# The last feed-forward of a GNN block: two tiles weighed inside the first part's loop, the first turning ahead of the last first product, and no filling products

## The reference

```python
input_acts = _gelu(jnp.einsum('bsd,nd->bsn', x, input_patterns))         # 256 of 256 kept
process_acts = _gelu(jnp.einsum('bsn,pn->bsp', input_repr, process_input_weights))
top_p_acts, top_p_idx = jax.lax.top_k(process_acts, K_PROCESS)           # 128 of 1024
sel_values = process_values[top_p_idx]
p_weights = jax.nn.softmax(top_p_acts, axis=-1)
agg_value = jnp.einsum('bsk,bskd->bsd', p_weights, sel_values)
output_acts = _gelu(jnp.einsum('bsd,od->bso', agg_value, output_input_weights))
out = jnp.einsum('bsk,bskm->bsm', top_o_acts, sel_patterns)              # 256 of 256 kept
```

## Time and profile before

| what | value |
|---|---|
| median of 3 runs | 1284.91 us (1284.19 to 1285.83) |
| the profiled execution's own time | 1289.82 us |
| its span (first to last instruction) | 1288.1 us |
| TensorE busy | 1219.5 us, 95% |
| VectorE busy | 547.9 us, 43% |
| ScalarE busy | 452.7 us, 35% |
| GpSimd busy | 227.7 us, 18% |
| the last feed-forward's first product | at 1162.14 us of the span |
| the last output product | at 1280.97 us of the span |

### The profile page before, as it was taken

The page is one execution under the profiler, slowest core; times in us unless marked ns, Lnnn a source line. Parts: engine busy times, 40 slices in busy tenths (PEclk is TensorE's granted clock), DMA queues, the critical chain, the costliest instruction groups (busy, mean ns, idle before and its releaser), DMA issues. The chain is left out here.

```text
span 1288.1 us, 19378 instructions
## 1 busy us (share of the span) xinstructions
PE 1219.5 (95%) x6528; PEld 814.0 (63%) x6529; DVE 547.9 (43%) x1535; ACT 452.7 (35%) x965; POOL 227.7 (18%) x227
## 2 busy tenths in 40 slices
PE   4999899999999899999999999999989999989898
PEld 2555476468448555478877887786555587564465
DVE  8999743433443344110000000001296345675784
ACT  6878533233223310011111111111123343338873
POOL 1000070030000008311111111111273000025540
PEclk9999899999999989999999999999998999999899
DMA  9300000000003300671165312564562010100011
GB/s 221 91 1 1 1 2 1 0 2 2 0 6 126 130 2 1 203 273 42 44 245 182 115 44 70 216 236 148 167 186 98 1 35 1 74 0 1 1 31 52
DMA packets 42978, 98.25 MB, mean 76 GB/s; under 512 B 4142, under 2 KB 6632, under 8 KB 41874
## 3 DMA queue, kind: packets, MB, share of 16 engines
q1 hardware_dynamic: 28642, 68.70, 16.0%
q0 software_dynamic: 6144, 16.45, 4.6%
q10 hardware_dynamic: 8112, 12.08, 2.6%
HBM read 81.02 MB, written 16.17 MB: 75 GB/s over the span
## 5 line engine op out<-in xcount | busy, mean ns | idle before, releaser
L498 PEld LDWEIGHTS psum<-sb_blk,sb_w_reg 128*128 128x128 f32 x1792 | 204.0, 192 | 12.8 <-issue 12.8
L498 PE MATMUL psum<-sb_blk,sb_w_reg 128*128 128x128 f32 x1792 | 205.2, 275 | 1.7 <-issue 1.7
L2145 PE MATMUL psum<-sb_z_reg_r,sb_hT_conv_r 125*125 125x512 f32 x385 | 156.9, 408 | 0.4 <-DVE sb_z_last L1262 0.4
L1434 DVE TENSOR_TENSOR sb_blk<-sb_blk,psum 128x256 f32<-128x256 f32 x56 | 23.6, 421 | 277.0 <-ACT sb_blk L955 277.0
L2145 PE MATMUL psum<-sb_htok_r,sb_hT_conv_r 125*125 125x512 f32 x285 | 112.9, 396 | 0.0
L498 PE MATMUL psum<-sb_hT_conv,sb_w_reg 128*128 128x416 f32 (+3 forms) x336 | 103.6, 465 | 0.8 <-ACT sb_hT_conv L532 0.8
L2235 PE MATMUL psum<-sb_w_reg,sb_blk 128*128 128x512 f32 x224 | 100.8, 592 | 0.0
L498 PEld LDWEIGHTS psum<-sb_hT_conv,sb_w_reg 128*128 128x128 f32 x336 | 63.8, 193 | 35.9 <-issue 33.0
L2145 PEld LDWEIGHTS psum<-sb_z_reg_r,sb_hT_conv_r 125*125 125x125 f32 x385 | 72.0, 187 | 18.0 <-issue 0.7
L2067 PE MATMUL psum<-sb_w_reg,sb_hT_conv 128*125 128x512 f32 x160 | 83.1, 613 | 0.0
L955 ACT ACTIVATE sb_blk<-psum 128x256 f32<-128x256 f32 x56 | 21.5, 384 | 162.9 <-PE psum L498 160.1
(11 more groups left out here) (452 smaller groups left out, 2002.3 us busy)
## 6 DMA issues: line engine op xcount, KB each, us to landing
sb_hT_conv<-w_expert SPq DMA_DIRECT2D x7, 2048.0 KB, 9.8
sb_w_reg<-w_expert SPq DMA_DIRECT2D x6, 2048.0 KB, 18.1
sb_hT_conv<-w_expert SPq DMA_DIRECT2D x7, 1024.0 KB, 12.4
slot_outs<-sb_blk ACTq DMA_DIRECT2D x28, 256.0 KB
sb_w_reg<-w_expert SPq DMA_DIRECT2D x6, 1024.0 KB, 19.9
sb_w_reg<-w_gnn SPq DMA_DIRECT2D x1, 4096.0 KB
sb_w_reg<-w_qkv SPq DMA_DIRECT2D x1, 3072.0 KB, 21.5
slot_outs<-sb_blk ACTq DMA_DIRECT2D x1, 2560.0 KB, 13.1
```

The source lines that it names most:

```text
L498: ins = e.matmul(out, l, r, start=(n == 0), stop=(n == len(pairs) - 1))
L1434: e.tensor_tensor(hidT[:, 2 * h:2 * h + 2, :].rearrange("p k n -> p (k n)"), silg[:, h, :], psum[:, 1 + h, HF:2 * HF], ALU.mult).then_inc( ...
L2145: ins = e.matmul(psum[0:TP, b, :], counts_at(l, 2 * i + n // NT)[:, s % HALF_T, :], z[s], start=(n == 0), stop=(n == len(pairs) - 1))
```

## The change

FIRST_PRODUCTS = 8. TensorE forms the first products of tiles 0 to 7, checks tile 0, forms those of tile 8 into banks 6 and 7, turns tile 0's weights, and forms those of tile 9 behind that turning. Both groups of filling products of this stage are gone. ScalarE loads and applies the exponentials of tiles 0 and 1 in step 8, ahead of the Gelu of tiles 8 and 9; counts below for tiles 0, 1 and 2 in steps 6, 8 and 10 (steps 7, 11 and the second part before); and copies tile 0's turned weights in step 10. VectorE does two parts of `vec_choose` per step, those of tiles 0, 1 and 2 in steps 5 to 10 (EARLY = 3), and weighs tiles 0 and 1 in steps 8 and 10. The second part's order inside a step is otherwise kept, from step t = 3 on.

```diff
--- before.py
+++ after.py
@@ -89,7 +89,8 @@
 N_PROC, D_PV, K_PROC = 1024, 256, 128
 REPLACED = -3.0e38
 
-EARLY, EARLY_FROM, CHOICE_PARTS = 2, 5, 4
+EARLY, EARLY_FROM, CHOICE_PARTS = 3, 5, 4
+FIRST_PRODUCTS = 8
 GROUPS = 6
 GROUP_AT = [n * N_PROC // GROUPS for n in range(GROUPS + 1)]
 CAND = 8 * GROUPS
@@ -533,6 +534,9 @@
             else:
                 e.activation(hT[:, :, tile(i)], view, func).then_inc(hT_in, 1)
 
+        def product_bank(n):
+            return n % 4 if n < 2 * FIRST_PRODUCTS else 6 + n % 2
+
         def every(t, first, gap):
 
             i, rest = divmod(t - first, gap)
@@ -981,7 +985,7 @@
 
         def act_signs(e, i, t, done):
 
-            e.activation(junk[:, 0 if t >= NT else 1, :], acts[:, i, :], ACT.Sign, bias=thr[:, i:i + 1], scale=-1.0,
+            e.activation(junk[:, 0 if t >= FIRST_PRODUCTS else 1, :], acts[:, i, :], ACT.Sign, bias=thr[:, i:i + 1], scale=-1.0,
                          accum_out=cnt[:, i:i + 1]).then_inc(done, 1)
 
         def act_exp(e, i):
@@ -993,6 +997,14 @@
         def act_bad(e, i):
             e.wait_ge(bad_mm, i + 1)
             e.copy(bad_i[:, i:i + 1], psum[0:1, 0, 0:1]).then_inc(bad_in, 1)
+
+        def act_turned_weights(e, i):
+            if i >= 2:
+                e.wait_ge(o_mm, i - 1)
+            for g in range(2):
+                e.wait_ge(w_turned, 2 * i + g + 1)
+                e.copy(wT[:, i % 2, 4 * g:4 * g + 4, :],
+                       psum[:, 1 + g, 0:4 * TP].rearrange("p (k n) -> p k n", k=4)).then_inc(wT_in, 1)
 
         def act_count_below(e, i):
             e.wait_ge(chosen_pool, BELOW + 2 * i)
@@ -1202,19 +1214,22 @@
             e.wait_ge(x_two, NT + 1)
             for t in range(NT + 2):
 
-                if t == NT:
+                if t == FIRST_PRODUCTS:
                     act_exp(e, 0)
                     act_exp(e, 1)
                     act_bad(e, 0)
-                if t >= EARLY_FROM + 2 and (t - EARLY_FROM - 2) % CHOICE_PARTS == 0:
-                    if t > NT:
-                        e.wait_ge(counted_a, NT)
-                    act_count_below(e, (t - EARLY_FROM - 2) // CHOICE_PARTS)
+                if t == NT:
+                    act_turned_weights(e, 0)
+                    act_bad(e, 1)
+                if t in (6, 8, 10):
+                    if t == 10:
+                        e.wait_ge(counted_a, NT - 1)
+                    act_count_below(e, (t - 6) // 2)
                 for i in of_tiles(t, 2):
                     e.wait_ge(thr_refined, i + 1)
                     e.wait_ge(counted_a, i + 1)
-                    if t >= NT:
-                        e.wait_ge(counted_c, t - NT + 1)
+                    if t in (8, 10):
+                        e.wait_ge(counted_c, (t - 6) // 2 + 1)
                     act_signs(e, i, t, counted_b)
                 for i in of_tiles(t, 1):
                     e.wait_ge(thr_guess, i + 1)
@@ -1224,16 +1239,12 @@
                 for i in of_tiles(t, 0):
                     for h in range(2):
                         e.wait_ge(proc_mm, 2 * i + h + 1)
-                        e.activation(acts[:, i, h * 512:(h + 1) * 512], psum[0:TP, (2 * i + h) % 4, :], ACT.Gelu,
+                        e.activation(acts[:, i, h * 512:(h + 1) * 512], psum[0:TP, product_bank(2 * i + h), :], ACT.Gelu,
                                      accum_out=act_sum[:, i, h:h + 1]).then_inc(acts_in, 1)
             for t in range(EARLY, NT + 5):
                 for i in of_tiles(t, 3):
-                    if i >= 2:
-                        e.wait_ge(o_mm, i - 1)
-                    for g in range(2):
-                        e.wait_ge(w_turned, 2 * i + g + 1)
-                        e.copy(wT[:, i % 2, 4 * g:4 * g + 4, :],
-                               psum[:, 1 + g, 0:4 * TP].rearrange("p (k n) -> p k n", k=4)).then_inc(wT_in, 1)
+                    if i >= 1:
+                        act_turned_weights(e, i)
                 for i in of_tiles(t, 4):
                     e.wait_ge(o_turned, i + 1)
                     if i >= 2:
@@ -2029,20 +2040,19 @@
                     e.wait_ge(chosen_pool, BELOW - 1)
                     e.wait_ge(ia_in, 6)
                     e.tensor_copy(places16, iota16).then_inc(v_own, v.up())
-                if t >= EARLY_FROM:
-                    vec_choose(e, *divmod(t - EARLY_FROM, CHOICE_PARTS))
-                if t == NT:
-                    vec_weigh(e, 0)
-            for part in range(NT + 3 - EARLY_FROM, EARLY * CHOICE_PARTS):
-                vec_choose(e, *divmod(part, CHOICE_PARTS))
-            vec_weigh(e, 1)
+                for later in range(2):
+                    part = 2 * (t - EARLY_FROM) + later
+                    if 0 <= part < EARLY * CHOICE_PARTS:
+                        vec_choose(e, *divmod(part, CHOICE_PARTS))
+                if t in (8, 10):
+                    vec_weigh(e, (t - 8) // 2)
             for t in range(EARLY, NT + 5):
                 for i in of_tiles(t, 5):
                     e.wait_ge(pat_mm, i + 1)
                     e.tensor_tensor(x_res[:, i, :], x_res[:, i, :], psum[0:TP, 6 + i % 2, :], ALU.add).then_inc(x_last, 1)
                 for i in of_tiles(t, 0):
                     for part in range(CHOICE_PARTS):
-                        vec_choose(e, i, part, i - 1 if i > EARLY else None)
+                        vec_choose(e, i, part, i - 1)
                 if t == NT:
                     vec_weigh(e, NT - 1)
 
@@ -2328,6 +2338,22 @@
             if c % 2 == 1 or c == IN_PAIRS - 1:
                 ins.then_inc(ia_mm, 1)
 
+        def pe_process(e, i):
+
+            for h in range(2):
+                n = 2 * i + h
+                if n >= 2 * FIRST_PRODUCTS + 2:
+                    e.wait_ge(acts_in, n - 1)
+                elif 4 <= n < 2 * FIRST_PRODUCTS:
+                    e.wait_ge(acts_in, n - 3)
+                group(e, psum[0:TP, product_bank(n), :], [(actsT[:, k, tile(i)], w_pi[:, k, h * 512:(h + 1) * 512])
+                                                          for k in range(2)]).then_inc(proc_mm, 1)
+
+        def pe_check(e, i):
+            e.wait_ge(bad_ready, i + 1)
+            e.wait_ge(bad_in, i)
+            e.matmul(psum[0:1, 0, 0:1], ones_col, bad[:, i:i + 1], start=True, stop=True).then_inc(bad_mm, 1)
+
         def pe_features(e, n, p, banks, done):
 
             for s in range(2):
@@ -2622,15 +2648,13 @@
 
             for i in range(NT):
                 e.wait_ge(ia_in, i // 4 * 2 + 2)
-            for i in range(NT):
-                for h in range(2):
-                    n = 2 * i + h
-                    if n >= 4:
-                        e.wait_ge(acts_in, n - 3)
-                    group(e, psum[0:TP, n % 4, :], [(actsT[:, k, tile(i)], w_pi[:, k, h * 512:(h + 1) * 512])
-                                                    for k in range(2)]).then_inc(proc_mm, 1)
-            e.wait_ge(acts_in, 2 * NT)
+            for i in range(FIRST_PRODUCTS):
+                pe_process(e, i)
+            e.wait_ge(acts_in, 2 * FIRST_PRODUCTS - 3)
             e.wait_ge(pv_in, 4)
+            pe_check(e, 0)
+            pe_process(e, FIRST_PRODUCTS)
+            e.wait_ge(acts_in, 2 * FIRST_PRODUCTS)
             for t in range(EARLY, NT + 5):
                 for i in of_tiles(t, 3):
                     e.wait_ge(weighed, i + 1)
@@ -2642,12 +2666,15 @@
                             ins = e.transpose(psum[:, 1 + g, k * TP:(k + 1) * TP], wexp[i % len(wexp)][:, c:c + 128],
                                               ident[0:TP, 0:TP])
                         ins.then_inc(w_turned, 1)
-                if t == EARLY + 1:
-                    pe_busy(e, 7, w_op[:, 0, :], 2)
+                if t == EARLY:
+                    for i in range(FIRST_PRODUCTS + 1, NT):
+                        pe_process(e, i)
                 for i in of_tiles(t, 5):
                     e.wait_ge(outT_in, i + 1)
                     if i >= 2:
                         e.wait_ge(x_last, i - 1)
+                    else:
+                        e.wait_ge(acts_in, 2 * NT)
                     group(e, psum[0:TP, 6 + i % 2, :], [(outT[:, i % 2, k, :], w_op[:, k, :])
                                                         for k in range(2)]).then_inc(pat_mm, 1)
                 for i in of_tiles(t, 4):
@@ -2658,11 +2685,7 @@
                                           ident[0:TP, 0:TP])
                     ins.then_inc(o_turned, 1)
                 for i in of_tiles(t, 2):
-                    e.wait_ge(bad_ready, i + 1)
-                    e.wait_ge(bad_in, i)
-                    e.matmul(psum[0:1, 0, 0:1], ones_col, bad[:, i:i + 1], start=True, stop=True).then_inc(bad_mm, 1)
-                if t == EARLY:
-                    pe_busy(e, 7, w_op[:, 0, :], 6)
+                    pe_check(e, i)
 
                 for i in of_tiles(t, 3):
                     e.wait_ge(wT_in, 2 * i + 2)
```

## The result

| | before | after |
|---|---|---|
| median | 1285.91 us (8 runs, 1282.44 to 1287.29) | 1291.85 us (8 runs, 1288.79 to 1298.11) |
| ratio after to before | | 1.0051, 95% interval 1.003 to 1.0073 |
| profiled execution: own time, span | 1289.82, 1288.1 us | 1289.28, 1287.5 us |
| first first product to end of the last output product | 1162.14 to 1282.95: 120.81 us | 1155.01 to 1282.35: 127.34 us |

The kernel became slower, by 0.51% or about 6.5 us by the ratio; the plain difference of the two medians is 5.94 us. The two profiled spans don't show it: the profiled execution of after reached the last feed-forward 7.1 us earlier, by a difference in the stages ahead of it that the change doesn't touch and that varies from one execution to the next. So all traces are compared here by the length of the last feed-forward, the last row of the table, which takes 6.53 us longer.

The account below looks back on a forecast made before the run. ScalarE's queue up to the second part's first Gelu was taken as the bound. Values starting 4.6 us late, plus 2.6 for the clock, less 0.5, gave 6.6: median 1284.91 to 1291.5 us, range 1286.5 to 1293.6.

Parts of the forecast that it names:

- ScalarE's queue and the loads: Before the second part's first Gelu: four function table changes in place of two, 1.29 us each, costing 2.6 us more.
- the rival of two extra drains: Each ScalarE table change waits for it to run empty: 2.3 us for two, 1293.8 us; chance 3 in 100.
- Waits of ScalarE: ScalarE waits 0.7 and 1.5 us for tile 9's product, 1.0 for the refinement; second part's first Gelu 4.8 late.
- The clock: TensorE's clock halves after both idle gaps, slowing tile 9's product and tile 1's values; 2.6 us at the values.
- The sum: At the start of tile 2's turning: 6.6 us late, with order and work behind it as before.
- What sets the joint before: In the kernel before, ScalarE's queue up to the second part's first Gelu ends last and starts tile 1's values.
- The other side: TensorE's filling was the path; tile 0's values, 2.0 us earlier, pull the stream along: 1282.9 us; 6 in 100.
- One gap or none at the low clock: TensorE's clock falls in one gap only (1288.9 to 1289.5 us, chance 0.13) or in neither (1286.9, chance 0.10).

Follow-up runs that it names:

- e8: Kernel before with tile 0's exponential moved to step 8, adding two table loads: last feed-forward 123.56 us, ratio 1.003.
- e3: Changed kernel with the exponentials of tiles 2 and 3 computed in step 8, two table loads fewer: last feed-forward 126.20 us, ratio 1.0042.
- e9: Kernel before with the count below of every odd tile of the second part one step later: last feed-forward 118.08 us, ratio 0.9973.
- e2: Kernel before with its eight filling products of this place taken out: last feed-forward 120.73 us, ratio 0.9986.
- e1: Changed kernel with filling products in both TensorE gaps, 8 before tile 0's turning, 6 behind tile 1's: last feed-forward 125.75 us, ratio 1.0033.
- e7: Changed kernel, tile 9's product right behind tile 8's, tile 1's weighing behind tile 9's refinement, second part's exponentials one step later: last feed-forward 128.76 us, ratio 1.0046.
- e6: Changed kernel, exponentials of tiles 2 and 3 in step 8, tile 9's product right behind tile 8's, tile 1's weighing behind tile 9's refinement: 120.93 us, ratio 0.9997.
- e5: Changed kernel with VectorE's weighing of tile 1 moved from step 10 to 11, behind tile 9's refinement: last feed-forward 125.58 us, ratio 1.0042.

## Why the prediction held

- **ScalarE's queue and the loads.** Right, and shown by e8 alone (2.72 for 2.6), with e3 in line with it (2.25 for 2.6). The drain behind each switch that the page of the Trainium skill (ScalarE: Activation LUTs, What ACT_TABLE_LOAD costs) adds is not in these traces: loads on L995 and L1242 hand over after 1.29 us, so the rival of two extra drains is out.
- **Waits of ScalarE.** For tile 9's product 0.7 and 1.5 were forecast, 0.95 and 1.03 came. For the refinement 1.0 was forecast, and it was 1.55. In step 5, taken as 0, the wait was 1.04 where it had been 0.68. VectorE's own start of a weighing was left out of the sum: it idled for 0.74 us between its choice for tile 1 and the weighing of tile 0, and for 0.71 ahead of that of tile 1. The first starts the first turning at 39.73 in place of the forecast 38.5, together with ScalarE's lateness from step 5; the second goes into the wait for the refinement. The Gelu thus came at 60.7 in place of 59.3.
- **The clock.** Both falls were forecast, and both low stretches too long: 4.9 and 3.8 us from the first work behind the gap, not 6.1. So the values of tile 1 took 5.16 us in place of 6.2. This error of 1.0 and the one above nearly cancel: turning of tile 2 at 67.18, forecast 66.9 (1229.0 less 1162.14).
- **The sum.** 6.6 us forecast, 6.53 in the traces, 0.51% by the ratio. That the sum is this close is partly luck. Two terms were each off by over 1 us, in opposite directions. And the forecast took all of it at the turning of tile 2, with the old spacing behind it; there the change is 6.98 us late, and 0.45 us come back behind it (60.16 to the end in place of 60.61).
- **What sets the joint before.** The prediction has ScalarE's queue end last there. The last wait ahead of the values of tile 1 was in fact that for VectorE's choice for tile 2, by 0.07 us. It made no difference to the sum, as the Gelu moved 6 us past it, but it means that a faster ScalarE would have gained nothing at the joint, as e9 shows.
- **The other side** (the filling was the path) is refuted by e2, where taking it out alone changed the length by 0.08 us, and by e1, where putting it back left 4.9 us of the loss. One gap or none at the low clock is out by the clock's rows.

## What to carry to other kernels

Before reordering two loops, add up the queue of the engine whose result the next stage waits for, the function table loads among it: an exponential moved between Gelus costs two loads, and here each was paid in full. A chain through filling products shows where the wait was, not what it costs; take them out alone to see. Where several waits lie on one queue, single mends can give less than they do together (here 4.43 us against 6.41): judge them together. And a time that didn't move can hide a gain and a loss of the same size, as in e2: look at what each instruction waited for.

## What was not expected of the hardware

TensorE's clock fell behind shorter gaps than the one of 4.05 us seen before: in e1 the granted clock was 0.97 in the last microsecond of a gap of 2.30 us and 0.50 in the next three, although five microseconds of solid products stood ahead of it. It also fell behind gaps of 2.66 us in e3 and of 1.97 us in e7, and held behind one of 2.07 us in e6, so the length of the gap alone doesn't tell. In the changed kernel it fell about 3 us into one gap and 4.5 us into the other. How long it stays low from the first work on varied too: 6.14 us before, 4.9 and 3.8 us after, and 3.2 in e5 behind the same gap of 8.29 us that gave 4.9 after. So a low stretch can be priced only within some 3 us from one sighting. The clock of e1 around that gap, in single microseconds:

```profile
1220.85:1221.85 1.00, 0.52 (x2) 1.00 0.00 0
1221.85:1222.85 1.00, 0.00 (x0) 1.00 0.00 0
1222.85:1223.85 1.00, 0.18 (x1) 0.97 0.00 0
1223.85:1224.85 1.00, 0.79 (x5) 0.50 0.00 0
...
1227.85:1228.85 1.00, 1.00 (x7) 1.00 0.00 0
```
